# A linear-attention and gated-LoRA block on one core: five pieces of the written instruction order moved

## What is computed

```python
q, k, v = sigmoid(x@Wq+bq), sigmoid(x@Wk+bk), x@Wv+bv          # 16 heads of 8
sink_in = n / sum_d((q+eps)*(cum(k)+eps));  src_out = n / sum_d((k+eps)*(cum(q)+eps))
cons_sink = sum_d((q+eps)*(cum(k*src_out)+eps)) / n
cons_src  = exp(clip(sum_d((k+eps)*(cum(q*sink_in)+eps)) / n, -1, 1))
vs = v * cons_src / cum(cons_src) * n
kv = cum(outer(k, vs));  attn = (q*sink_in/n @ kv) * sigmoid(cons_sink) @ Wo + bo
h  = layernorm(x + attn);  z = layernorm(h + gelu(h@W1+b1)@W2 + b2)
x2 = layernorm(x + z)
gate = softmax(x2@gate_w + gate_b); the two largest are kept, weight = their sum
out = layernorm(x2 + sum over the two experts e of weight * (relu(x2@wi + bi + lora_e(x2))@wo + bo))
```

## Time and profile before

| | |
|---|---|
| median of 3 executions | 429.71 us (428.76 to 429.75) |
| the profiled execution's own time | 428.76 us, its span 427.0 us |
| busy: TensorE, VectorE, GpSimd, ScalarE | 383.5, 336.7, 225.5, 207.4 us |
| chain that ended last, by engine | PE 38%, DVE 25%, issue 15%, POOL 11%, DMA 5% |

### The profile page before, as it was taken

One profiled execution on the slowest core, in us unless ns is written; L12 is line 12 of the kernel. 1 busy time (PEld: TensorE's weight loads), 2 busy tenths in 40 slices (PEclk: granted clock), 3 DMA queues, 4 the chain that ended last, 5 costly groups with the idle time before them and its releaser, 6 DMA issues.

```text
span 427.0 us, 6466 instructions
## 1 busy us (share of the span) xinstructions
PE 383.5 (90%) x2114; PEld 266.8 (62%) x2114; DVE 336.7 (79%) x795; ACT 207.4 (49%) x375; POOL 225.5 (53%) x263
## 2 busy tenths in 40 slices
PE   8897889878999999899998998999998998799991
PEld 3555656475757775686658773877478665775651
DVE  3559956597799898989799889988898979843632
ACT  2230233427554575627751783557553673265541
POOL 2026243963488328933794369733993389554211
PEclk9999999999999999999999999999999999999997
DMA  8245008200280007200550028000820053000000
GB/s 258 106 89 134 1 2 186 61 1 1 45 203 2 0 2 186 86 0 2 118 154 2 0 51 221 2 0 8 209 60 0 2 135 87 0 2 25 0 26 25
DMA packets 19857, 26.58 MB, mean 62 GB/s; under 512 B 1648, under 2 KB 9968, under 8 KB 19824
## 3 DMA queue, kind: packets, MB, share of 16 engines
q1 hardware_dynamic: 19680, 25.96, 23.8%
q10 hardware_dynamic: 144, 0.21, 0.2%
HBM read 7.29 MB, written 2.10 MB: 22 GB/s over the span
## 4 chain that ended last, share of the span: by engine, by line
PE 38%; DVE 25%; issue 15%; POOL 11%; DMA 5%; ACT 2%; SPq 2%; POOLq 0%; DVEq 0%; ACTq 0%
POOL prod L828 7%; PE pY L432 6%; PE pB L352 5%; DVE kv L1022 5%; PE pY L512 4%; PE pG L422 4%; DVE cum_kv L1028 4%; DMA vb<-vs 3%; PE pG L501 3%; DVE cum_ks L918 2%; DVE cum_q L918 2%; SPq L291 2%; DMA xT<-x_t 2%; PE pG L494 2%; DVE gel L1119 2%
## 5 line engine op out<-in xcount | busy, mean ns | idle before, releaser
L828 POOL TENSOR_TENSOR prod<-cum_kv,q_fac 128x512 f32<-128x512 f32 x64 | 93.4, 1466 | 29.2 <-DVE cum_kv L1028 26.2
L405 PEld LDWEIGHTS pO<-s_wor,prod 128*128 128x128 f32 x512 | 62.6, 191 | 26.0 <-POOL prod L828 18.1
L405 PE MATMUL pO<-s_wor,prod 128*128 128x128 f32 x512 | 67.6, 279 | 8.9 <-POOL prod L828 8.8
L1022 DVE TENSOR_TENSOR kv<-k,vb 128x512 f32<-128x512 f32 x64 | 53.4, 835 | 6.8 <-DMA vb<-vs 6.8
L815 POOL TENSOR_TENSOR var_eps<-mv,s_con 128x4 f32<-128x4 f32 x32 | 11.0, 343 | 74.1 <-DVE mv L1042 74.1
L1028 DVE TENSOR_TENSOR_SCAN cum_kv<-p_ones,cum_kv,kv 128x512 f32<-128x512 f32 x32 | 40.5, 1275 | 0.6
L1028 DVE TENSOR_TENSOR_SCAN cum_kv<-p_ones,kv 128x512 f32<-128x512 f32 x32 | 38.5, 1214 | 0.5
L741 ACT ACTIVATE relu<-pG,s_att 128x512 f32<-128x512 f32 x28 | 19.2, 685 | 32.9 <-PE pG L494 32.7
L512 PEld LDWEIGHTS pY<-s_moe,gel 128*128 128x128 f32 x256 | 31.1, 192 | 6.1 <-issue 4.3
L432 PEld LDWEIGHTS pY<-s_ffn,gel 128*128 128x128 f32 x256 | 30.9, 192 | 3.8 <-issue 3.8
L818 POOL TENSOR_TENSOR rstd<-var_eps,s_con 128x4 f32<-128x4 f32 x32 | 32.9, 1030 | 0.0
(11 more groups left out here) (164 smaller groups left out, 801.5 us busy)
## 6 DMA issues: line engine op xcount, KB each, us to landing
vb<-vs SPq DMA_DIRECT2D x64, 256.0 KB, 4.6
xT<-x_t SPq DMA_DIRECT2D x8, 256.0 KB, 4.8
xt<-x SPq DMA_DIRECT2D x8, 256.0 KB, 5.0
out<-y SPq DMA_DIRECT2D x8, 256.0 KB, 2.3
s_moe<-moe_w SPq DMA_DIRECT2D x1, 836.0 KB, 10.3
s_wor<-wo_rep SPq DMA_DIRECT2D x1, 512.0 KB, 8.2
s_ffn<-ffn_w SPq DMA_DIRECT2D x1, 512.0 KB, 8.8
s_con<-consts SPq DMA_DIRECT2D x1, 502.0 KB, 4.5
```

The costliest lines, as they stand in the source:

```text
L405: mm = pe.matmul(pO3[:, s, :], prod[:, m % 4, s * P:(s + 1) * P], s_wor[:, m, :], start=False, stop=(m == DH - 1), skip_group_check=True)
L828: pool.tensor_tensor(prod[:, m % 4, :], cum_kv[t.par][:, m, :], q_fac[t.par][:, :], ALU.mult).then_inc(prod_ready, 1)
L1022: dve.tensor_tensor(kv[:, m % 3, :], k[t.par][:, :], vb[:, m, :], ALU.mult).then_inc(kv_ready, 1)
```

## The change

Five pieces are moved; no instruction is added or removed, except that the loads of xT stand at another step. The lines of the changed kernel are numbered one to three higher.

```diff
--- before.py
+++ after.py
@@ -309,9 +309,10 @@
                 a, b, c, d = s.plus(1), s, s.plus(-1), s.plus(-2)
                 A, B, C, D = a.exists(), b.exists(), c.exists(), d.exists()
                 if B: spread_vs(b, 4); spread_vs(b, 5); spread_vs(b, 6)
-                if A and a.n >= 2: load_xT(a)
+                if A and a.n == 2: load_xT(a)
                 if A and a.n >= 1: load_xt(a)
                 if B: spread_vs(b, 7)
+                if A and a.plus(1).exists() and a.n >= 2: load_xT(a.plus(1))
                 if A: spread_vs(a, 0); spread_vs(a, 1)
                 if D: store(d)
                 if A: spread_vs(a, 2); spread_vs(a, 3)
@@ -615,7 +616,7 @@
                 if C: logits(c)
                 if B: reduce_out(b, 5); reduce_out(b, 6); reduce_out(b, 7)
                 if D: expert_out(d, 0)
-                if A: head_sums(a, 0, True); head_sums(a, 0, False); project_v(a)
+                if A: project_v(a); head_sums(a, 0, True); head_sums(a, 0, False)
                 if s.n == 1: keep_busy(1, pG[1])
                 if D: expert_out(d, 1); expert_out(d, 2)
                 if A: denominators_T(a, 0)
@@ -787,8 +788,10 @@
                 if A: q_out(a)
                 if D: relu(d, 3)
                 if A: k_out(a)
-                if C: normalise(c, 2); x2T_out(c); gate_exp(c)
-                if A: v_out(a); spread_denominators(a, 0)
+                if C: normalise(c, 2); x2T_out(c)
+                if A: v_out(a)
+                if C: gate_exp(c)
+                if A: spread_denominators(a, 0)
                 if B: normalise(b, 0)
                 if A: spread_denominators(a, 1)
                 if B: h_out(b); gelu(b, 0); gelu(b, 1)
@@ -1194,27 +1197,20 @@
                 if C: gate(c, 3)
                 if A: normal_denominators(a)
                 if C: gate(c, 4); gate(c, 5); sum_exp(c)
-                if A: sink(a)
-                if C: gate(c, 6)
-                if A: cumulate_sink(a)
-                if C: gate(c, 7)
+                if C: gate(c, 6); gate(c, 7); gate(c, 8); inverse_sum_exp(c)
+                if A: sink(a); cumulate_sink(a)
+                if C: gate(c, 9)
                 if A: source(a); k_times_cum_q(a, 1); cumulate_source(a)
-                if C: gate(c, 8); inverse_sum_exp(c)
+                if C: gate(c, 10)
                 if A: q_times_cum_k(a, 1)
-                if C: gate(c, 9)
+                if C: gate(c, 11)
                 if D: expert_residual(d)
-                if C: gate(c, 10)
-                if A: conserved(a)
-                if C: gate(c, 11)
-                if A: clip_source(a)
-                if C: masked_lora(c, True)
-                if A: prefix_e(a)
-                if C: gate(c, 12)
-                if A: allocation(a)
+                if A: conserved(a); clip_source(a)
+                if C: gate(c, 12); masked_lora(c, True)
+                if A: prefix_e(a); allocation(a)
                 if C: gate_total(c); masked_lora(c, False)
-                if A: inverse_cum_e(a); source_factor(a); sink_factor(a)
+                if A: inverse_cum_e(a); source_factor(a); sink_factor(a); values(a)
                 if D: moments(d, 3)
-                if A: values(a)
                 if B: moments(b, 1)
                 if A: query_factor(a); outer_product(a, 0); cumulate_kv(a, 0)
                 if A: outer_product(a, 1)
```

## The result

The changed kernel takes 431.31 us (median of 6 executions, 430.42 to 432.37), the kernel before 429.2 (median of 6, 428.6 to 429.75). The ratio is 1.005, with a 95% interval of 1.0037 to 1.0063: 2.1 us slower.

The account below looks back on a forecast made before the run. Bound by TensorE and VectorE waiting for each other, then TensorE, then VectorE with GpSimd. -0.2 - 0.74 - 5 x 0.8 + 5 x 1.15 = +0.8 us: 429.6 profiled, 430.5 median; range 426.8 to 433.6, the forecast's own 428.3 to 431.7.

Parts of the forecast that it names:

- the lag: GpSimd running late behind the moved fourth moments: 1.15 us later in each step from 3 to 7, bounds 0 and 2.06.
- Gate steps and projection: From cum_q to kq: cum_qs 1.5 us sooner, kq held by GpSimd's addition; 0.8 us gained in each of steps 2 to 6.
- Delta and alloc: Step 1: ud comes 1.1 us sooner and TensorE's wait for it goes, 0.74 us once; nothing in steps 2 to 6.
- now only the first does: Step 1: of two GpSimd additions that blocked delta and alloc in turn, only the first still blocks; ud 1.1 us sooner.
- Fourth moments: Behind vs: VectorE pays nothing, GpSimd's inverse_std(d, 3) starts 2.06 us later; 1.15 us lost in each step from 3 to 7.
- of its idle 0.95 the projection has taken 0.86, so 0.1 is left as cover: TensorE ahead of the head sums: only 0.1 us of idle time covers GpSimd's last product, 1.25 us late.
- rival 2: VectorE loses races to GpSimd's products at kv: delay 2.1 us a step, 435.2 us, slower; chance 0.12.
- The late store: SyncE's store of y ahead of vb 2 to 7: they come 0.95 us later, vb 2 just about when kv 2 wants it.
- Rival 1: GpSimd's 2.09 us of idle time absorb the lag, 0.3 us a step left: 426.3 us, faster; chance 0.22.
- xT: Load a step ahead: TensorE's 1.73 us wait goes, project_q starts where it does now; price 0, bounds 0 to 0.3 a step.
- Rival 3: The gate's gain doesn't come (rden_x late or kq meets the second addition), 0.1 a step: 434.0 us, slower; chance 0.08.

Follow-up runs that it names:

- e5: e1 with GpSimd's addition h_residual cut to 4 of 512 columns, leaving out nearly all of that addition; 422.86 us, ratio 0.9852 to the kernel before.
- e3: The kernel before with only VectorE's gate steps moved; 429.5 us, ratio 1.0002.
- e9: e3 with gate step 9 (pick) moved from behind cum_qs to behind cum_ks; 426.87 us, ratio 0.9946 to the kernel before.
- e10: The changed kernel with only the value projection back behind both groups of head sums on TensorE; 441.93 us, ratio 1.0291 to the kernel before.
- e8: e1 with gate_sum ahead of u1, ud directly behind e_pref and alloc behind rcum_e on VectorE; 425.2 us, ratio 0.9901 to the kernel before.
- e2: The kernel before with only the fourth moments moved behind vs; 436.04 us, ratio 1.0151.
- e1: The changed kernel with the fourth moments put back ahead of vs; 426.0 us, ratio 0.9918 to the kernel before.
- e4: The kernel before with only xT loaded a step ahead; 429.49 us, ratio 0.9999.
- e11: e1 with cum_ks moved ahead of kq of pair 1 on VectorE; 423.8 us, ratio 0.988 to the kernel before.
- e6: The changed kernel with x_b2n and x2c ahead of inverse_std(d, 3) on GpSimd; 434.75 us, ratio 1.0136 to the kernel before.
- e7: e1 with x_b2n (shifted_x) moved ahead of inverse_std(d, 3) on GpSimd; 429.13 us, ratio 0.9997 to the kernel before.
- e12: The edits of e8 and e11 together on e1; 423.81 us, ratio 0.9869 to the kernel before.

## Why the prediction was right and wrong

I forecast 430.5 us, "the same" within 0.3% but with its range up to 431.7; measured were 431.31, 0.5% slower. That the number came so close is luck in part. In the profiled executions step 1 gave 0.9 us less than forecast and the gate 0.3 less, while the lag cost 5.4 and not 5.75, and that by another route.

**Gate steps and projection: right in size and mechanism, but not each for itself.** Forecast 0.8 us in each of steps 2 to 6, measured 0.76, 0.71, 0.76, 0.71 and 0.77. rden_x was 0.13 us sooner behind cum_q (0.15 forecast), q_sink 0.38 (0.4), cum_qs 1.37 (1.5), and kq was held by h_residual as foreseen, 1.29 us; e5 shows that this hold costs 3.1 us. The Trainium skill (SBUF — State Buffer, section Who interferes with whom) has the port kept by the instruction that issued first; kq's 1.29 against 0.69 us without the addition agree. Not seen: the gain hangs on gate step 9 asking 0.15 us ahead of the addition (e3, e9), and on the projection and v_out moving together (e10).

**Delta and alloc: wrong.** The step that failed is "now only the first does": I took alloc as the only operation that the additions still block. gate_sum, next in VectorE's queue, met the second one, TensorE still waited 0.62 us for ud, and step 1 as a whole gave 0.04 us and not 0.94. These 0.9 us are the largest part of the difference between the forecast +0.8 and the +1.6 of the profiled execution. e8 moves gate_sum away and gets 0.88.

**Fourth moments: the size right, the route wrong.** GpSimd's wait was 5.35 us (5.4 forecast), the last product 1.38 late behind vs in step 4 and 0.9 in steps 2 and 3 (1.25 forecast), the loss a step 0.91, 0.87, 1.38, 1.39 and 0.9 in the tail, 1.09 on average against 1.15. Wrong is where it lands: "of its idle 0.95 the projection has taken 0.86, so 0.1 is left as cover". No such cover counts, with or without the projection (e2, e10). GpSimd's late x_b2n and products stand in front of kv 0 and of kv 4 or kv 7, VectorE falls behind, and with it cum_q, on which all of the next step hangs. So rival 2 had the mechanism, one lost race on the chain, and its sign came (two kv of over 1.5 us in each of steps 2 to 5), but its price of 2.1 us a step was too high: 0.9 to 1.4 were measured. The late store, which I priced at nothing because vb 2 would land just about when kv 2 wants it, was forecast 0.95 us later and came 0.97 later; it costs a wait of 0.26 at kv 2. Prod 0 is 2.1 us later and not 1.5. Rival 1, that idle time absorbs the lag, is refuted: B in e1 against the changed kernel.

**xT: right.** The wait is gone and worth nothing (e4, 0.9999). **Rival 3** didn't come; e3 and e10 show two ways in which the gain is lost.

**The rest.** The medians differ by 2.1 us and the profiled executions by 1.6; the others of the changed kernel ran at a mean granted clock of 0.990 to 0.996. I can't attribute the remaining 0.5 us.

## What to carry to other kernels

When an operation is moved out of reach of a GpSimd addition, ask what stands next in its queue: however small, it inherits the wait (gate_sum, 128x4, 1.27 us), and an order can win or lose everything on 0.1 us. What ran there without a wait is a running sum that reads its ones from PSUM (e11); one with both inputs in SBUF was held up like the rest (e_pref). A delay of an engine off the critical path is not covered by idle time further down, when the two engines hold each other up: look for the first operations that its late work will now meet, and for the transfers that stand behind it. Two moves that look independent (here the value projection and the exponential's table load) can be one, so price a piece also with its partner left out.

## What was unexpected in the hardware

- The granted clock fell in single stretches, in step 1 of e1 for no cause in the edit, since e1 differs from the changed kernel only from step 2 on. Windows of e1 and of e2 (columns as above):

```profile
92.00:98.00 6.00, 5.53 (x36) 4.03 (x35) 5.62 (x18) 2.20 (x3) 2.44 (x4) 1.00 0.00 0
98.00:107.00 9.00, 7.18 (x36) 5.41 (x37) 7.17 (x19) 6.32 (x11) 2.83 (x4) 0.81 0.00 1
```

```profile
220.00:230.00 10.00, 8.10 (x30) 4.80 (x29) 9.86 (x17) 4.66 (x8) 8.37 (x9) 0.83 0.23 68
```

A mean of 0.81 means that part of the stretch ran at 1.2 and not 2.4 GHz. TensorE had been busy for 5.53 of the 6 us ahead of it in e1 and for 8.97 of 10 in e2. In e1 step 1 took 22.56 us and not 21.59, in e2 step 4 24.62 and not 22.97. The changed kernel shows 1.00 from 98 to 107 us with a nearly equal load (7.03 of 9), while e5, e6, e7, e8 and e10 show 0.81 there as e1 does. What tips it stays open. Such kernels are better compared step by step than by the median alone.

- alloc, which took 1.21 us beside x_bo, took 0.13 in e8, 0.08 us after x_b2n had begun (110.79 and 110.71), and the next operation, v_scale, took 1.12. So not every small operation that the trace puts inside an addition waits. e12 repeats it (alloc 0.13 us, 0.08 behind the start of x_b2n). kv 4 above won and lost with the same 0.05 us, so below 0.1 us the starts in the trace may not be the order in which the two were served; no run shows it.
